# Two-layer decoder on one core: phases 1 and 2 as one list of work without a barrier, and scores of the last cross attention as one unit

## Time and profile before

| what | value |
|---|---|
| timed runs | 3619.38 to 3625.34 us, median 3624.97 |
| the profiled execution | 3628.03 us, span 3626.1 |
| mean granted clock of TensorE | 0.969 |
| busy: PE, DVE, ACT, POOL | 3344.5, 2625.4, 2283.5, 1022.4 us |
| instructions | 59862 |

### The profile page before, as it was taken

The page is one execution under the profiler, slowest core; times in us unless marked ns, Lnnn a source line. Parts: engine busy times, 40 slices in busy tenths (PEclk is TensorE's granted clock), DMA queues, the critical chain, the costliest instruction groups (busy, mean ns, idle before and its releaser), DMA issues.

```text
span 3626.1 us, 59862 instructions
## 1 busy us (share of the span) xinstructions
PE 3344.5 (92%) x20706; PEld 2528.1 (70%) x20706; DVE 2625.4 (72%) x7153; ACT 2283.5 (63%) x4067; POOL 1022.4 (28%) x1576
## 2 busy tenths in 40 slices
PE   5999999999999848999999999999999876999998
PEld 4677777777777636777777777777777655766664
DVE  5688888888888644677777777777777534788876
ACT  3677777777777622456666555556556543677776
POOL 2244444444444422222222322222223110000000
PEclk8999999999999979999999999999999877999999
DMA  7654545445544021444444444444444421011010
GB/s 193 101 95 84 88 96 107 84 88 95 107 84 82 17 82 53 84 80 77 86 92 94 94 88 88 90 89 93 92 87 88 73 44 62 12 36 35 25 35 24
DMA packets 203403, 283.27 MB, mean 78 GB/s; under 512 B 48929, under 2 KB 131874, under 8 KB 194274
## 3 DMA queue, kind: packets, MB, share of 16 engines
q1 hardware_dynamic: 203106, 279.46, 38.2%
HBM read 179.49 MB, written 96.73 MB: 76 GB/s over the span
## 4 chain that ended last, share of the span: by engine, by line
PE 71%; ACT 11%; DVE 7%; DMA 5%; issue 4%; SPq 1%; POOL 1%; PEld 0%; POOLq 0%; ACTq 0%; PEldq 0%; DVEq 0%
PE ps L829 35%; PE ps L1003 8%; PE ps L978 7%; PE ps L1201 5%; PE ps L1017 5%; ACT q_stack L1669 5%; PE ps L953 3%; DMA qk_scratch<-parts 3%; ACT pt L1686 2%; PE ps L984 1%; PE ps L1077 1%; PE ps L888 1%; PE ps L1028 1%; DMA k_stack<-qk_scratch 1%; DVE nmax L1351 1%
## 5 line engine op out<-in xcount | busy, mean ns | idle before, releaser
L1686 ACT ACTIVATE pt<-ps 128x512 f32<-128x512 f32 x1280 | 735.9, 598 | 346.7 <-PE ps L1003 338.8
L1889 POOL TENSOR_SCALAR_AFFINE_SELECT pt<-pt 128x256 f32<-128x256 f32 x1024 | 392.1, 419 | 704.9 <-ACT pt L1686 704.9
L978 PE MATMUL ps<-k_stack,q_stack 96*128 96x512 f32 (+3 forms) x2048 | 547.2, 338 | 42.3 <-ACT q_stack L1669 11.8
L1358 DVE CUSTOM_DVE_ANT_0 ps<-ps,future 128x512 f32<-128x512 f32 (+3 forms) x1024 | 481.7, 515 | 141.9 <-PE ps L978 138.8
L1003 PE MATMUL ps<-q_stack,k_stack 100*128 100x512 f32 (+3 forms) x2048 | 538.6, 345 | 29.3 <-ACT q_stack L1669 23.4
L1003 PEld LDWEIGHTS ps<-q_stack,k_stack 100*128 100x128 f32 x2048 | 351.5, 195 | 124.9 <-ACT q_stack L1669 37.2
L978 PEld LDWEIGHTS ps<-k_stack,q_stack 96*128 96x128 f32 x2048 | 355.6, 194 | 103.2 <-ACT q_stack L1669 18.8
L1351 DVE TENSOR_REDUCE nmax<-ps 128x1 f32<-128x512 f32 (+2 forms) x768 | 354.4, 502 | 92.0 <-PE ps L984 91.0
L1895 POOL TENSOR_TENSOR rs<-rs 128x4 f32<-128x4 f32 x96 | 97.1, 1012 | 1062.0 <-DVE rs L1394 1062.0
L1669 ACT ACTIVATE q_stack<-ps 4x512 fp32r<-4x512 f32 x512 | 300.8, 588 | 64.7 <-PE ps L992 56.5
L1017 PE MATMUL ps<-pt,v_ones 128*32 128x512 f32 (+3 forms) x4096 | 312.1, 446 | 5.7 <-POOL pt L1889 5.3
(11 more groups left out here) (278 smaller groups left out, 7958.6 us busy)
## 6 DMA issues: line engine op xcount, KB each, us to landing
qk_scratch<-parts SPq DMA_DIRECT2D x64, 1024.0 KB, 5.5
q_stack<-qk_scratch SPq DMA_DIRECT2D x384, 128.0 KB, 4.9
k_stack<-qk_scratch SPq DMA_DIRECT2D x384, 128.0 KB, 5.6
gate_of<-gate_scratch SPq DMA_DIRECT2D x128, 256.0 KB, 5.6
x_mid<-x_ring SPq DMA_DIRECT2D x32, 512.0 KB, 3.9
x_ring<-x_mid SPq DMA_DIRECT2D x32, 512.0 KB, 5.3
x_ring<-in_x SPq DMA_DIRECT2D x16, 512.0 KB, 3.8
out_dram<-x_ring SPq DMA_DIRECT2D x16, 512.0 KB, 2.9
```

The source lines that it names most:

```text
L978: done = e.matmul(bank(bank_of[piece])[:, at:at + width], a.q[0:96, base + h, t * P:(t + 1) * P], a.k[0:96, base + h, 0:width], start=a.la ...
L1358: done = e.tensor_tensor_reduce(src, src, future[:, SEQ - width:SEQ], -1.0, 3e38, ALU.add, ALU.min, nmax[:, g % 2, to:to + 1])
L1686: e.activation(dst, src, ACT.Exp).then_inc(exp_up.sem)
L1889: done = e.affine_select(out=blk, in_=blk, compare_op=ALU.is_ge, fill=0.0, base=0, pattern=[[0, 2], [1, P]], channel_multiplier=-1)
```

## The change

Phases 1 and 2 become one list. `START` sets phase 2's due times 1210 us behind those of phase 1, the due times of both are written anew (periods 73.001, 95.398 and 32.104 in place of 70.45, 91.45 and 31.45), and `merged` sorts both with the pieces of `AHEAD`, which hold what prologue 2 did: five loads of 768 KB with the weights of two experts each (`w2`), which SP issues once a group's transposed scores of batch 15 are done, since the load goes into memory of phase 1's key stack; the router (`rt`), the low-rank factors (`low`), their six products (`lw`), zeroing and ones (`z`), and the projection (`wo`). Within each phase the order on every engine is as before, but for neighbours that had the same due time. The drain and barrier between the phases, prologue 2 and the 20 dummy matmuls in it are gone; `WARM` stays.

The expert weights are laid out expert by expert; the second attention shares value, probability and output buffers with the first; the write-back's buffer is partly `oT`, so a copy of one waits for the reader of the other. The banks are taken over both phases from one set, `wide`, `late` and `narrow`.

In phase 3, `a_parts` holds the high and low part of a key block side by side. A scores matmul with the high part of x reads both, 128 columns, one with the low part reads 64: 16 matmuls. DVE copies the second half, adds it to the first, and goes on as before. The query bias moves into `offset`, formed in the prologue by four DVE operations (two multiplications, two additions of 128x512); two copies on ACT go. `co_b` is added by a new GpSimd piece `tb x1`, and its matmul pair in `cw` goes.

```diff
+START = {1: 0.0, 2: 1210.0, 3: 0.0}
+LATE = 1145.0
+SOONER = 8.0
@@ TABLE
-    1: (70.45, {
+    1: (73.001, {
...
-    2: (91.45, {
+    2: (95.398, {
...
-    3: (31.45, {
+    3: (32.104, {
...
+AHEAD = {
+    "tensor": {"lw": [1267.1, 1267.2, 1267.3, 1267.4, 1267.5, 1267.6]},
+    "scalar": {"w2": [1139, 1154, 1168, 1171, 1186], "rt": [1110], "low": [1189],
+               "lw": [1267.3, 1267.4, 1267.5, 1267.6, 1267.7, 1267.8], "wo": [1340], "z": [1280, 1285]},
+    "vector": {"w2": [1141, 1156, 1170, 1173, 1188], "rt": [1111], "low": [1191],
+               "z": [1268.1, 1271.5], "lw": [1267.4, 1267.5, 1267.6, 1267.7, 1267.8, 1267.9], "wo": [1341]},
+    "gpsimd": {"z": [1268, 1271]},
+    "sync": {"w2": [1133, 1148, 1162.5, 1162.6, 1179], "rt": [1106], "low": [1182], "wo": [1272]},
+}
...
+def merged(when):
+    out = {engine: {**when[1][engine], **ahead_of(engine), **when[2][engine]} for engine in ENGINES}
...
-                    out[engine][piece] = b * period + row[n]
+                    out[engine][piece] = START[ph] + b * period + row[n]
...
+        both = merged(when)
+        turns = {12: {engine: in_turn(both, engine) for engine in ENGINES},
+                 3: {engine: in_turn(when[3], engine) for engine in ENGINES}}
...
-        for ph in (1, 2, 3):
+        for ph, part in ((1, 12), (3, 3)):
...
-        score_banks, turned_banks, other = Banks([0, 1]), Banks([2, 3]), Banks([4, 5, 6, 7])
-        for piece in turns[1]["tensor"]:
...
+        halls = Banks(range(8))
+        score_banks, turned_banks = halls.only([0, 1]), halls.only([2, 3])
+        wide, late, narrow = halls.only([4, 5, 6, 7]), halls.only([0, 1, 2, 3]), halls.only([4, 5])
+        for piece in turns[12]["tensor"]:
...
+            first = kind in ("xv", "xq", "xs", "xp", "xo") or piece in when[1]["tensor"]
             if kind in ("S", "N"):
-                take(score_banks, piece, 2)
-            elif kind in ("T", "PV", "O", "gr", "gt", "gg"):
-                take(turned_banks, piece, 2)
+                take(score_banks, piece, both)
+            elif kind in ("T", "gr", "gt", "gg") or kind in ("PV", "O") and not first:
+                take(turned_banks, piece, both)
...
+            elif first:
+                take(late if both["tensor"][piece] > both["tensor"]["dn", 0, 0, 0] - SOONER else wide, piece, both, 2 if kind in ("tc", "tm") else 1)
...
@@ cw
-                    ops.append((ones[:, :], co_b[:, :]))
@@ cs
-                        ops = []
-                        for c in range(CT):
-                            ops += three(ch[:, c, rows], cl[:, c, rows], a_h[:, c, keys], a_l[:, c, keys])
-                        done = product(e, bank(bank_of[piece])[:, t * CTX:(t + 1) * CTX], ops)
+                        both = bank(bank_of[piece])[:, 2 * t * CTX:2 * (t + 1) * CTX]
+                        done = None
+                        for c, part in ((0, ch), (0, cl), (1, cl), (1, ch)):
+                            wide = part is ch
+                            done = e.matmul(both if wide else both[:, 0:CTX], part[:, c, rows],
+                                            a_parts[:, c, b, :, :].rearrange("p a k -> p (a k)") if wide else a_parts[:, c, b, 0, :],
+                                            start=wide and c == 0, stop=wide and c == 1)
@@ vector, prologue 3
+                        for n in range(2):
+                            cols = slice(n * 512, n * 512 + 512)
+                            e.wait_ge(bq_up, n + 1)
+                            e.wait_ge(keys_lo, 12)
+                            e.tensor_tensor(tile32[:, n, :], bank(4 + n), seen[:, cols], ALU.mult).then_inc(mine.up())
+                            e.wait_ge(*mine.now)
+                            e.tensor_tensor(offset[:, cols], offset[:, cols], tile32[:, n, :], ALU.add).then_inc(mine.up())
@@ ce
-                    e.tensor_tensor(sc3[:, :, :], bank(bank_of[piece])[:, 0:TT * CTX].rearrange("p (t k) -> p t k", t=TT),
-                                    key_row(q_bias), ALU.add).then_inc(cs_add.sem)
+                    halves = bank(bank_of[piece]).rearrange("p (t a k) -> p t a k", t=TT, a=2)
+                    e.tensor_copy(sx3[:, :, :], halves[:, :, 1, :]).then_inc(mine.up())
+                    e.wait_ge(*mine.now)
+                    e.tensor_tensor(sc3[:, :, :], halves[:, :, 0, :], sx3[:, :, :], ALU.add).then_inc(cs_add.sem)
...
-                    e.tensor_tensor(sc3[:, :, :], sc3[:, :, :], key_row(unseen), ALU.add).then_inc(mine.up())
+                    e.tensor_tensor(sc3[:, :, :], sc3[:, :, :], key_row(offset), ALU.add).then_inc(mine.up())
@@ scalar, w2
+                    e.wait_ge(w2_in[i], 16)
+                    e.activation(w2_h[:, cols], w2_raw[:, cols], ACT.Copy).then_inc(ahead_hi.sem)
```

More of the change, by code:

```diff
@@ L574, in leaves @@
             kind, key = piece[0], piece[1:]
+            if kind == "lw":
+                return ahead_lo[piece], "vector", piece
             if kind in ("tc", "qk", "xq", "xo", "cw"):
@@ L937, in tensor @@
                     warm(bank(5)[:, 0:P], 16)
-                if kind == "prologue" and key[0] == 2:
-                    e.wait_ge(w_lo.sem, W3_READY - len(W3.chunks) - 2)
-                    warm(bank(7)[:, 0:P], 20)
                 if kind in ("prologue", "end"):
```

572 lines of the change are left out of this document (355 added, 217 removed), and 262 rows, old and new, of the table TABLE.

## The result

The changed kernel takes 3585.39 us (median of four runs, 3582.85 to 3588.25), where four runs of the kernel before give 3623.81: a ratio of 0.9896, 95% interval [0.9883, 0.9909]. That is 38 us faster. The forecast was 78 us faster, 3547. The measured time lies in the stated range, near its upper end, but the gain is only half of the likeliest one. The profiled execution took 3585.21 us, span 3583.5, so between the two profiled executions 42.6 us are gained.

A forecast was written before the change was run, and what follows sets the result against it. The prediction took TensorE (PE), busy for 92% of the span, to bound the kernel. 3628.0 - 75 + 18.5 - 25.8 + 2.7 + 1.3 = 3549.7, less 3.1, gave some 3547 us; range 3510 to 3592.

The forecast's parts named there:

- Steady phase 1 (+18.5): Batches 2 to 15: a changed bank makes PE wait 1.32 us longer before tm v0, 18.5 us slower in all.
- Rival (a): Steady phase 1: the late bank costs nothing, as VectorE slides along; 3528 us, chance 0.15.
- The boundary (-75): Between phases 1 and 2: without the barrier, phase 2's first attention (tc a1 0) starts 75 us earlier; bounds 50 to 91.
- 17.3 us "/0.89": Boundary, first part: PE work moved ahead of batch 15's last transposed score, at 89% busy, puts that event at 1248.
- 95.6 us: Boundary, second part: PE work from that score to tc a1 0, at a 0.93 busy share, takes 103 us.
- rival (c): Boundary: the two chains hinder each other on in-order engines, so 75 becomes 41 and the time 3581; chance 0.14.
- so the copy finds its data there: Boundary: each 768 KB weight load lands in 5.7 us, before ScalarE's copy, due 6 us behind the issue.
- rival (d): Boundary: ScalarE waits in order for each of five loads, up to 20.5 us each; slower, 3649 us, chance 0.04.
- Phase 3 (-25.8): Phase 3: fewer score matmuls and no bias pair save 1.6 us in each of 16 batches; VectorE's added copy mostly hidden.
- rival (b): Phase 3: VectorE or the GpSimd lock holds the old period; 3573 us, or 3585 with the full lock; chance 0.12.
- Prologue 3 (+2.7): Phase 3's prologue: four added VectorE operations of 0.68 us, in a chain PE waits for, cost 2.7 us.
- Phase 2 (0): Phase 2 from tc a1 0 on: it runs in its steady order, which the change leaves alone; 0 us.

The follow-up runs named there:

- banks_old: The changed kernel, with phase 1's pieces other than scores in the PSUM banks they had before the change: 3574.1 us, ratio 0.9854.
- before_wait: The kernel before, with tm v0 of batches 2 to 15 also waiting for VectorE's add of xs 7 two batches back: 3649.45 us, ratio 1.0066.
- no_warm: The changed kernel without the dummy matmuls around the boundary (89 in the table): 3577.76 us, ratio 0.9864.
- rt_late: The changed kernel, with the split of the router's weights 15 us later on ScalarE and VectorE: 3581.01 us, ratio 0.9877.
- double_split2: The changed kernel, with one more 1.75 us VectorE operation before each of the five expert-weight split subtractions, run again: 3595.95 us, ratio 0.9917.
- tail: The changed kernel, with the six low-rank products spread over 9 us and the zeroing of the new stacks 10 to 12 us later: 3585.39 us, ratio 0.9892.
- two_ops: The changed kernel, with phase 3's cross attention 2 mask applied by two VectorE operations, not four; wholly hidden batches get other weights: 3578.76 us, ratio 0.9873.
- banks_rt: The changed kernel with phase 1's old banks and the later router split, dummies kept: 3570.73 us, ratio 0.9850.
- best2: The changed kernel with phase 1's old banks, no dummies around the boundary and the later router split: 3562.61 us, ratio 0.9828.

## Why the prediction was half right

**Steady phase 1 (+18.5): right, in sign, place and size.** The trace shows 1.12 us of idle before tm v0 and a period longer by 1.29 us; banks_old and before_wait bear it out from both sides. Rival (a) falls.

**The boundary (-75): the direction right, the size wrong; this is the step that failed.** It was measured at -46 (234.5 less 1.3 for batch 15's own bank wait, against 279.4). What failed is how PE's work was turned into time: 17.3 us "/0.89" ahead of the last transposed score, and 95.6 us behind it at a busy share of 0.93, taken "between the 0.89 of that stretch and the 0.965 of steady phase 1". The measured shares are 0.85 before PV of batch 15's last group and 0.90 behind. The sum treated PE's work as what bounds, with waits as a tax. no_warm shows that it isn't: 22 us of PE work taken away shorten the stretch by 8.3. What bounds with it is the order of pieces on VectorE and ScalarE: rt_late finds 4 us in one load that ScalarE waits for, double_split2 finds that 7.0 us more on VectorE cost 9.7. That is rival (c)'s mechanism, two chains that hinder each other in fixed orders, and near its price: it said 41 won, 46 were. That the two lie so near may be luck, since its 41 is no more than the length of the old hole. I gave it 0.14. Its argument, that "each step now queues behind expert work", was left as a rival when it should have been in the sum: none of the splits (18 us of VectorE, which I had counted) had a place in the time.

Of the 29 us that are missing, the runs put only the router's 4 to a single place. In the second half most of the idle time stands at its end (the changed kernel):

```profile
1280.40:1366.00 85.60, 81.81 (x511) 66.35 (x510) 61.18 (x128) 36.47 (x64) 35.31 (x33) 1.00 0.17 47
1366.00:1398.30 32.30, 24.30 (x111) 17.57 (x112) 16.21 (x37) 7.55 (x16) 10.52 (x7) 0.84 0.12 33
```

tail, the one run that moved pieces there, won nothing. So the step that failed is known, and which piece costs how much of the rest stays open.

A term of that step was wrong as well: "76 dummy matmuls that the warm-up table still names, at no more than 1.27/9 = 0.14 us each". The row that I divided had been cut short by the stretch in which it was read. Whole, it has ten entries, for the five dummies that the table names there:

```profile
1228.39 1.38 PE L888 MATMUL ps<-ident 128*128 128x128 f32 x10
```

So a dummy is two rows. In the changed kernel the 76 are 152 rows, busy for 19.1 us where I had 10.6:

```profile
L1021 PE MATMUL ps<-ident 128*128 128x128 f32 x152 | 19.1, 276 | 0.0
```

That is 8.5 of the 18.1 us of busy time too many. Of the rest a part is the clock, 0.96 where I had taken every price at full clock, although the row of the old kernel for 1343.5 to 1427 has 0.98 and that for 1245.7 to 1294 has 0.96; how large a part was not measured. But this miscount does not explain the missing 29 us: the forecast had charged 10.6/0.93 = 11.4 us of time for the dummies, and taking all of them out won 8.3.

I also wrote "so the copy finds its data there". For the five large loads this is right (a median of 4.7 us, no wait), and rival (d) falls with it. I overlooked the smallest load, the router's.

**Phase 3 (-25.8): right in kind, 1.20 of the 1.61 us per batch.** The PE work saved was 1.70 us per batch, a little more than the 1.61 forecast (25.8/16; its two terms, 0.9 and 0.69, make 1.59). The copy "is hidden" was wrong: 0.5 us per batch came back as waits, through the exponential's place in ScalarE's order, as two_ops shows. This is the first half of rival (b), VectorE in place of PE as the bound, at a smaller price than its 25.8. It makes some 5 of the 9 us by which phase 3 fell short. The other 4 come from counting 16 equal batches: between the first down products of the last four batches there are 31.8, 27.9 and 26.9 us before and 31.3, 27.9 and 26.9 after, so next to nothing is won in them.

The second half of (b), the lock between GpSimd and VectorE, did not come in phase 3. GpSimd's and VectorE's timelines in phase 3:

```profile
3287.76 2.42 POOL L2065 TENSOR_TENSOR x_ring<-x_ring,co_b_rows 128x1024 f32<-128x1024 f32 x1 [7.10 <-PE ps L1074]
```

```profile
3287.88 1.53 DVE L1720 SCALAR_TENSOR_TENSOR ang<-tr,fc,ps 128x512 f32<-128x512 f32 x2
3289.33 1.28 DVE L1492 SCALAR_TENSOR_TENSOR xl<-ps,xh 128x512 fp32r<-128x512 f32 x2
```

The add falls where it was expected, and the operations beside it, with one input in PSUM, take 1.53 and 1.28 us as they did before (1.53 at 3322.45, 1.28 at 3323.89). The Trainium skill, "SBUF — State Buffer" (section "SBUF: two separate sides"), puts the lock on VectorE operations with two SBUF inputs; the trace agrees, since none of those shown here has two and none is longer.

**Prologue 3 (+2.7)**: PE's wait there is 8.90 us in place of 5.53, +3.4. Right in kind; most of the rest of the 5.5 us lies ahead of it, in PE's wait for the load and split of the weights, which the change leaves alone (32.28 us in place of 29.86).

**Phase 2 (0)**: 4.9 us were gained that no part of the change explains; the last section has where.

## What to carry to other kernels

When two phases with fixed orders are laid over each other, add up the work of the busiest engine for a lower bound of the time only; then walk the other engines' orders, and price every piece put among a chain of short dependent steps (a split, a wait for a small load) at its own length, unless the trace shows a wait right behind it. When a step gets longer by one operation, follow every instruction that stands behind its reader on that reader's engine, not only the data. And a planner that picks buffers from due times can cost more than its new order gains: compare, for each buffer, the last reader before and after.

## What the runs showed of the hardware that was not expected

The last batch of phase 2 has the same work in both kernels, but takes 78.00 us before and 72.00 after. Busy time by stretch, kernel before and then changed kernel:

```profile
2870.50:2948.50 78.00, 67.75 (x374) 48.66 (x374) 39.20 (x162) 38.50 (x68) 12.86 (x33) 0.72 0.33 45
```

```profile
2842.90:2914.90 72.00, 61.25 (x372) 44.48 (x372) 38.80 (x162) 38.40 (x68) 12.86 (x33) 0.81 0.35 49
```

The granted clock is 0.72 in one and 0.81 in the other; VectorE, ScalarE and GpSimd do the same. In other runs the batch took 72.0 (tail, banks_rt), 75.4 (rt_late) and 76.5 us (no_warm). Even two_ops, which is the changed kernel up to the end of phase 2, took 75.3 there at a clock of 0.75. So a loosely filled stretch gives or takes some 6 us with its clock and waits, from kernel to kernel and in part from one execution to the next; what decides was not tested. Part of a gain won earlier can be lost there: no_warm had won 9.3 us by PV of batch 16 and had 5.3 left at PV of batch 31.

At the boundary, too, waits and clock go together. Around 1242 us the lower level of the clock shows in the matmuls themselves (PE's timeline of the changed kernel):

```profile
1242.11 0.63 PE L963 MATMUL ps<-eh,w_lo 128*128 128x512 f32 x1
1242.54 0.63 PE L963 MATMUL ps<-el,w_hi 128*128 128x512 f32 x1
...
1252.22 0.40 PE L963 MATMUL ps<-eh,w_lo 128*128 128x512 f32 x1
1252.45 0.40 PE L963 MATMUL ps<-el,w_hi 128*128 128x512 f32 x1
```

They start 0.43 us apart at 1.2 GHz and 0.23 apart at 2.4; busy time by stretch has the granted clock:

```profile
1241.60:1244.20 2.60, 2.60 (x8) 1.74 (x6) 2.39 (x13) 0.67 (x2) 0.00 (x0) 0.50 0.00 0
1252.00:1253.40 1.40, 1.40 (x9) 1.12 (x8) 1.40 (x4) 0.36 (x1) 0.00 (x0) 1.00 0.00 0
```

The first pair comes 4 us behind a wait of 1.91 us on ScalarE (PE's start at 1238.31), in a stretch in which PE had many short waits. Over the whole boundary the changed kernel has a clock of 0.96 with dummies and no_warm 0.93 without, but banks_rt with them and best2 without them both have 0.94; in either pair the dummies cost more than they give.
